# Activation transposes on TensorE in fp32, or by transposing DMAs of fp16 halves

## What is computed

```python
q = _layer_norm(query, ln1_g, ln1_b)
qh = (q @ wq + bq).reshape(Bq, Sq, H, hd)
kh = (context @ wk + bk).reshape(Bq, Sc, H, hd)
vh = (context @ wv + bv).reshape(Bq, Sc, H, hd)
scores = jnp.einsum('bqhd,bkhd->bhqk', qh, kh) / sqrt(hd)   # masked: key k only for query >= k
probs = jax.nn.softmax(scores, axis=-1)
o = jnp.einsum('bhqk,bkhd->bqhd', probs, vh).reshape(Bq, Sq, Dm)
x = query + o @ wo + bo
h = _layer_norm(x, ln2_g, ln2_b)
return x + jax.nn.gelu(h @ w1 + b1, approximate=False) @ w2 + b2
```

## Time and profile before

| | |
|---|---|
| median of three runs | 2116.74 us (2114.98 to 2117.86) |
| span of the profiled execution | 2112.4 us |
| median of the runs less that span | 4.3 us |
| TensorE busy | 1975.8 us (94% of the span) |
| VectorE busy | 1304.6 us (62%) |
| ScalarE busy | 589.0 us (28%) |
| GpSimd busy | 466.0 us (22%) |
| DMA moved | 51.30 MB, mean 24 GB/s |

### The profile page before, as it was taken

How to read it: one execution, slowest core, us unless ns; L and a number is a source line. 1 busy time by engine, 2 the same in 40 slices (tenths; PEclk the granted TensorE clock), 3 DMA queues, 4 the chain that set the end, 5 groups by cost and what they waited for, 6 DMA issues and landing times.

```text
span 2112.4 us, 26940 instructions
## 1 busy us (share of the span) xinstructions
PE 1975.8 (94%) x10454; PEld 1003.4 (47%) x10454; DVE 1304.6 (62%) x1972; ACT 589.0 (28%) x820; POOL 466.0 (22%) x380
## 2 busy tenths in 40 slices
PE   4769999999999999999999999999999999999999
PEld 2434445444454544545455444544444454454544
DVE  5876666655656675666666566666655667556642
ACT  3544323222232312223232222313223231222311
POOL 2530131311212141211412023131121214111110
PEclk9879999999999999999999999999999999999999
DMA  7210000101000010000101000010100001000000
GB/s 254 62 28 1 21 20 1 41 0 40 2 11 30 1 41 1 21 20 6 36 1 40 1 21 21 1 40 1 41 1 11 30 1 41 1 21 20 1 21 20
DMA packets 27647, 51.30 MB, mean 24 GB/s; under 512 B 2536, under 2 KB 4112, under 8 KB 27536
## 3 DMA queue, kind: packets, MB, share of 16 engines
q1 hardware_dynamic: 27536, 49.58, 7.1%
...
## 4 chain that ended last, share of the span: by engine, by line
PE 73%; DVE 16%; issue 5%; ACT 3%; DVEq 2%; DMA 0%; POOL 0%; SPq 0%; POOLq 0%; ACTq 0%
PE ff_ps L1190 25%; PE ff_ps L989 23%; PE at_ps L989 15%; PE at_ps L1109 4%; PE at_ps L1032 4%; DVE ssum L927 3%; DVE arena L962 3%; PE at_ps L1133 2%; DVE arena L711 2%; DVEq L688 2%; DVE xhat L707 2%; DVE act_T L711 1%; DVE arena L976 1%; ACT L590 1%; ACT arena L590 1%
## 5 line engine op out<-in xcount | busy, mean ns | idle before, releaser
L1190 PE MATMUL ff_ps<-w_all,arena 128*128 128x512 f16 x3072 | 707.4, 380 | 32.0 <-DVE arena L711 27.7
L989 PE MATMUL ff_ps<-arena,w_all 128*128 128x512 f16 x3072 | 708.5, 381 | 11.9 <-issue 10.3
L1190 PEld LDWEIGHTS ff_ps<-w_all,arena 128*128 128x128 f16 x3072 | 297.8, 98 | 374.2 <-DVE arena L711 30.3
L989 PEld LDWEIGHTS ff_ps<-arena,w_all 128*128 128x128 f16 x3072 | 299.9, 98 | 357.4 <-issue 26.7
L645 ACT ACTIVATE arena<-ff_ps,b1p,scales 128x512 f32<-128x512 f32 x256 | 199.1, 778 | 891.8 <-PE ff_ps L989 803.0
L711 DVE SCALAR_TENSOR_TENSOR arena<-arena,scales 128x512 f16<-128x512 f32 x256 | 285.2, 1114 | 9.1
L485 POOL TENSOR_TENSOR arena<-arena,rsum 128x1024 f32<-128x1024 f32 x64 | 122.7, 1948 | 723.3 <-DVE rsum L930 723.3
L421 POOL TENSOR_TENSOR rstd<-ve,minus_half 128x1 f32<-128x1 f32 x128 | 90.6, 708 | 709.7 <-DVE ve L692 701.4
L962 DVE TENSOR_SCALAR arena<-arena,scales 128x512 f16<-128x512 f32 x256 | 160.1, 625 | 69.3 <-ACT arena L645 69.3
L711 DVE SCALAR_TENSOR_TENSOR arena<-at_ps,arena 128x512 f16<-128x512 f32 x188 | 123.8, 686 | 110.8 <-ACT arena L596 58.5
L989 PE MATMUL at_ps<-wo_hi,act_T 128*128 128x512 f16 x512 | 162.3, 379 | 1.5 <-DVE act_T L711 1.5
...
## 6 DMA issues: line engine op xcount, KB each, us to landing
x_sb<-in_x SPq DMA_DIRECT2D x64, 256.0 KB, 2.6
out_x<-arena SPq DMA_DIRECT2D x64, 256.0 KB, 2.3
w_all<-in_L_xattn_w SPq DMA_DIRECT2D x6, 1024.0 KB, 14.8
arena<-in_L_xattn_w SPq DMA_DIRECT2D x2, 1024.0 KB, 15.0
v_sb<-v_sb SPq DMA_DIRECT2D x6, 192.0 KB, 3.0
arena<-in_ctx SPq DMA_DIRECT2D x1, 1024.0 KB, 5.5
arena<-in_L_xattn_wk SPq DMA_DIRECT2D x1, 1024.0 KB, 8.1
arena<-in_L_xattn_wv SPq DMA_DIRECT2D x1, 1024.0 KB, 8.0
```

The lines of the kernel that those rows point to most:

```text
L989: last = nc.tensor.matmul(out_ap, s, m, start=(i == 0), stop=(i == n - 1))
L1190: last = nc.tensor.matmul(ff2_ps[:, t, :], pair[:, s, rows], m[:, j], start=(j == 0 and i == 0), stop=(j == NJ - 1 and i == 2))
```

## The change

All 64 fp32 transposes of a slot (16 for T, 32 for Z, 16 for H) are taken off TensorE. T, Z and H now split the data where it lies, with tokens on the partitions, and a transposing DMA moves both halves at once:

- T and H: ScalarE copies `xhat` to the high half in `xhl[:, t, 0]`, VectorE subtracts it from `xhat` into `xhl[:, t, 1]`; then SP issues one `dma_start_transpose` of 128 tokens x 1024 fp16 columns (256 KB) into `act_T` or `hT`.
- Z: the same with `probs[t]`, 1024 columns to each half in `phl[:, t % 2]`, so one DMA of 128 tokens x 2048 fp16 columns (512 KB) a tile, written over `probs[t]` itself.
- `xhl` and `phl` share the memory of `qT`. `phl` has two buffers, so ScalarE's Z2 and Z3 wait for the moves of Z0 and Z1.
- SP waits for each low half, then issues the move; in program order stand four T moves, four Z moves, the x loads of tiles 0 to 2, the H move of tile 0, the x load of tile 3, the other H moves, and the output stores.
- TensorE waits for the moves: at Q0 for the four of T, at V0 and V2 for two of Z each, at FF1(0) of the next slot for the four of H.
- `xhat` is free again when VectorE has made its low half.
- The plan moves: T at 2, 3, 4, 5; Q from 7; S and E one later; Z at 20 to 23; V0 and V1 at 24, V2 and V3 at 26; O at 27 to 30; H at 30 to 33 as before but for H1 and H2, one later.

```diff
-    2: [("T", 0)], 4: [("T", 1)], 5: [("T", 2), ("T", 3)],
-    6: [("Q", 0)], 7: [("Q", 1)], 8: [("Q", 2)], 9: [("Q", 3)],
-    10: [("S", 0)], 12: [("S", 1)], 13: [("S", 2)], 15: [("S", 3)],
-    16: [("E", 0), ("E", 1), ("E", 2), ("E", 3)],
-    20: [("Z", 0)], 21: [("Z", 1)], 22: [("V", 0), ("V", 1)],
-    23: [("Z", 2)], 24: [("Z", 3)], 25: [("V", 2), ("V", 3)],
-    26: [("O", 0)], 27: [("O", 1)], 28: [("O", 2)], 29: [("O", 3), ("H", 0)],
-    30: [("H", 1)], 31: [("H", 2)], 33: [("H", 3)],
+    2: [("T", 0)], 3: [("T", 1)], 4: [("T", 2)], 5: [("T", 3)],
+    7: [("Q", 0)], 8: [("Q", 1)], 9: [("Q", 2)], 10: [("Q", 3)],
+    11: [("S", 0)], 13: [("S", 1)], 14: [("S", 2)], 16: [("S", 3)],
+    17: [("E", 0), ("E", 1), ("E", 2), ("E", 3)],
+    20: [("Z", 0)], 21: [("Z", 1)], 22: [("Z", 2)], 23: [("Z", 3)],
+    24: [("V", 0), ("V", 1)], 26: [("V", 2), ("V", 3)],
+    27: [("O", 0)], 28: [("O", 1)], 29: [("O", 2)], 30: [("O", 3), ("H", 0)],
+    31: [("H", 1)], 32: [("H", 2)], 33: [("H", 3)],
...
+            def move_normed(c, t):
...
+                sp.wait_ge(t_lo, 4 * c + t + 1)
+                sp.sem_inc(moves_begun, 1)
+                sp.dma_start_transpose(act_blocks[:, :, t * P:(t + 1) * P],
+                                       xhl[:, t].rearrange("p a n -> p (a n)")).then_inc(t_moved[t], 16)
+
+            def move_probs(c, t):
+
+                sp.wait_ge(z_lo, 4 * c + t + 1)
+                sp.sem_inc(moves_begun, 1)
+                sp.dma_start_transpose(pT_blocks[t],
+                                       phl[:, t % 2].rearrange("p a n -> p (a n)")).then_inc(z_moved[t], 16)
+
+            def move_hidden(c, par, t):
...
+                sp.wait_ge(h_lo, 4 * c + t + 1)
+                sp.sem_inc(moves_begun, 1)
+                sp.dma_start_transpose(hT_blocks[par][:, :, t * P:(t + 1) * P],
+                                       xhl[:, t].rearrange("p a n -> p (a n)")).then_inc(h_moved[t], 16)
...
+                if attn:
+                    if not first:
+                        for t in range(TT):
+                            move_normed(c, t)
+                    for t in range(TT):
+                        move_probs(c, t)
+                    for t in range(TT - 1):
+                        load_next(t)
+                    move_hidden(c, par, 0)
+                    load_next(TT - 1)
+                    for t in range(1, TT):
+                        move_hidden(c, par, t)
...
+                if kind == "T":
+                    act.wait_ge(ln_out, 8 * c + t + 1)
+                    wait(act, h_moved[t], 16 * c)
+                    nc.scalar.activation(xhl[:, t, 0], xhat[:, t % 2, :], ACT.Copy).then_inc(t_hi, 1)
...
+                    act.wait_ge(p_norm, 4 * c + t + 1)
+                    if t < 2:
+                        wait(act, z_moved[t + 2], 16 * c)
+                    else:
+                        act.wait_ge(z_moved[t - 2], 16 * c + 16)
+                    nc.scalar.activation(phl[:, t % 2, 0], probs[t], ACT.Copy, scale=PROB_SCALE).then_inc(z_hi, 1)
...
+                nc.vector.tensor_tensor(xhl[:, t, 1], xhat[:, t % 2, :], xhl[:, t, 0], ALU.subtract).then_inc(t_lo, 1)
...
-            def transposes(source, bank, done):
-                for k in range(KT):
-                    last = nc.tensor.transpose(bank[:, k * P:(k + 1) * P], source[:, k * P:(k + 1) * P],
-                                               ident[:, :])
-                last.then_inc(done, 1)
...
                         if t == 0:
-                            pe.wait_ge(t_lo, 4 * c + 4)
+                            for n in range(TT):
+                                pe.wait_ge(t_moved[n], 16 * c + 16)
...
+                        if t % 2 == 0:
+                            for n in range(2):
+                                pe.wait_ge(z_moved[t + n], 16 * c + 16)
...
                         if g == 0:
-                            pe.wait_ge(h_lo, 4 * c)
+                            for n in range(TT):
+                                pe.wait_ge(h_moved[n], 16 * c)
```

More of the change, by code:

```diff
@@ L381, in move_values @@
                     sp.dma_start(v_sb[SC:P, a, even, :], v_sb[0:SC, a, even, :]).then_inc(v_moved, 16)
+            def move_normed(c, t):
+                if t == 0:
+                    wait(sp, o_ps, 4 * c)
+                    sp.sem_inc(moves_begun, 1)
[9 more added lines that the diff above has]
+            def move_hidden(c, par, t):
+                if t == 0:
+                    wait(sp, ff1_done, NJ * c + (-NJ))
+                    sp.sem_inc(moves_begun, 1)
+                    if isinstance(c, int) and c == 1:
+                        sp.wait_ge(conv_lo, len(conversions))
+                sp.wait_ge(h_lo, 4 * c + t + 1)
+                sp.sem_inc(moves_begun, 1)
+                sp.dma_start_transpose(hT_blocks[par][:, :, t * P:(t + 1) * P],
+                                       xhl[:, t].rearrange("p a n -> p (a n)")).then_inc(h_moved[t], 16)
+            for t in range(2):
+                move_normed(0, t)
             move_values(0, slice(0, 2))
+            for t in range(2, TT):
+                move_normed(0, t)
             move_values(1, slice(2, BATCH))
@@ L388, in slot, with load_next @@
             def slot(c, par, attn, ff, batch):
-                if not isinstance(c, int) or c < NCHUNK - 1:
-                    for t in range(TT):
+                first = isinstance(c, int) and c == 0
+                loads = not isinstance(c, int) or c < NCHUNK - 1
+                def load_next(t):
+                    if loads:
                         sp.wait_ge(x1_set, 4 * c + t + 1)
                         sp.dma_start(x_sb[:, t], x_tiles[4 * c + (TT + t)]).then_inc(x_loaded[t], 16)
+                if attn:
[10 more added lines that the diff above has]
+                        move_hidden(c, par, t)
                 if ff:
@@ L907, in step @@
                         dve.wait_ge(h_hi, 4 * c + t + 1)
-                        rows = slice(t * P, (t + 1) * P)
-                        low(hT[par][:, 1, :, rows], tiles, 1.0, hT[par][:, 0, :, rows], h_lo)
+                        nc.vector.tensor_tensor(xhl[:, t, 1], xhat[:, t % 2, :], xhl[:, t, 0], ALU.subtract
+                                                ).then_inc(h_lo, 1)
                         if t < 2:
@@ L1052, in _ @@
                                              for k in range(KT)]).then_inc(kv_ps, 1)
-            for t in range(2):
-                T_step(0, t)
             pe.wait_ge(wv_out, KT)
```

113 lines of the change are left out of this document (40 added, 73 removed), and 4 rows, old and new, of the table PLAN_FIRST.

## The result

The kernel after takes 2150.3 us (median, 2144.4 to 2154.3) against 2117.3 us of before on the same chip: a ratio of 1.016, 95% interval 1.014 to 1.018. The forecast was slower by 5.7% (2238 us); it is slower by 1.6%. The sign came out and most of the mechanism, the size did not: of +121 us between the spans, +40 were there. The profiled span is 2152.6 us. Between the medians the difference is 33 us, less than the 40 between the spans, because the profiled execution of after is the slowest of its four (2154.3 us).

What follows compares the result with a forecast made beforehand. VectorE's chain and its handover at Q0 bound the kernel; odd slots 128.9 us (+5.6), even 136.0 (+8.9), seven pairs +101, slots 0 and 1 +13 and +8, last -1: +121, so 2238 us; own range 2170 to 2330, overall 2100 to 2430.

Steps and rivals of the forecast that it cites:

- X: Time of one T or H move with waits and wake-up: 4.6 us (2.85 to 8.5), of which 4.4 landing.
- Z: As a time, one move of the probabilities with waits and wake-up: 7.15 us (3.85 to 17), of which 6.9 landing.
- step 4: V0 and V2 wait for the Z moves through two buffers, together 7.5 us per slot.
- H3's move is hidden: Between O3 and Q0: VectorE's chain goes on under FF1(0)'s wait, so only T3's move delays Q0.
- What bounds the kernel: At the handover to Q0: TensorE is nearly full, but Q0 starts when VectorE's chain, ending with T3's low half, lets it.
- Removed work: On TensorE: 64 transposes, 7.0 us per slot, some 105 us in 15 slots; also FF2(8)'s wait of 1.93 us.
- rival A: Moves run as fast as HBM loads: 2093 us, or 2170 at an SBUF copy's pace; chance 0.20.
- its second price: Moves at an SBUF copy's pace, 3.75 us for T and H, 5.75 for the probabilities: 2170 us.
- The formula: Waits of V0 and V2 per slot: twice the probabilities' move time less 6.8 us, 7.5 us together.
- Clock: TensorE's idle stretches bring the lower clock level: 1.5 us per odd and 2.5 per even slot (bounds 0 and 5).
- The start and the end: Slot 0 +13 us (0 to 25), slot 1 +8 (0 to 12), last slot -1.
- rival B: Slow or queued moves on one queue, 7 us for T and H, 12 for the probabilities: 2451 us; chance 0.20.

Runs made afterwards that it cites:

- e4: after with matmuls whose result nobody reads ahead of FF1(0)'s wait (18) and Q0's (10): 2122.8 us, 1.004 of before.
- e6: after with Q, S and E one position later in the written order: 2194.9 us, 1.034 of before.
- e5: before with its transposes kept and only the written order of work changed to that of after: 2078.5 us, 0.982 of before.
- e1: after with T and H back on TensorE in fp32, only the probabilities (Z) moved by DMA: 2047.0 us, 0.968 of before.
- e12: after with every Z move issued twice in series: 2427.6 us, 1.147 of before.
- e8: after with H's last move (H3) issued twice in series: 2179.6 us, 1.030 of before.

## Why the prediction was right, and where it was wrong

The step that failed is the size of the moves, X and above all Z, and with it step 4, V's waits: 7.5 us per slot forecast, 1.2 and 2.1 measured. That alone is some 82 us in seven pairs of slots, and the forecast for the pairs was 82 us too high. A second step, "H3's move is hidden", failed as well; the shorter moves hid that in even slots.

**What bounds the kernel.** Right in even slots: VectorE's chain and the handover at Q0. T3's doubled move came out one to one at Q0 (3.2 us for 3.1), and Q0 stayed at 36.6 to 36.8 us when TensorE was filled (e4) or given more work ahead of it (e6). In odd slots TensorE counts as well: with the filler Q0 came 1.4 us earlier.

**Removed work.** Right: 3.5 of the 7.0 us of transposes per slot are seen from e5 to e1, with V's wait of 1 us against them, and the order gave 2.1 us where 1.98 were counted. The other 3.5 us, T's and H's, stood ahead of Q0, where after has TensorE wait.

**Moves.** The term that failed. X was taken as 4.4 us to land and Z as 6.9, a quarter above copies inside SBUF by a slope through 64 and 192 KB. Measured: T 3.1, H 3.2 (4.3 to 4.9 for the last two, which queue), Z 4.4. With the 0.25 us of waking that is X = 3.4 and Z = 4.65, between the point from which rival A decides (3.1 and 4.4, no change) and its second price at the pace of a copy inside SBUF (3.75 and 5.75, 2170 us), and the time, 2150, lies between theirs. The surcharge of a quarter for short pieces had no row behind it. The slope had two rows, but they are for 64 and 192 KB: from 256 to 512 KB the landing grew by 1.3 us, not by 2. The Trainium skill, "Advanced Engine Details and Errata", section "X-Bar Transpose (TRN2)", has transposing DMAs as fast as regular ones: by these rows nearly so, 3.1 us against 2.6 for 256 KB loaded from HBM. In the Trainium skill's "VectorE: DVE Perf Modes", "The three transpose paths" has 1309 ns for one 128x128 block; here eight blocks land in 3.1 us, 0.39 per block, the figure that it gives for TensorE. TensorE's own fp32 transposes took 0.11 us per block here (eight in 0.87).

**V's waits.** The other half of the same failure, and nearly the whole miss. From the end of one block of matmuls to the start of the next, V0 waits 0.9 us and V2 0.2 (odd) or 1.2 (even), so 1.2 and 2.1 per slot. The formula with the landing as measured, 2 x 4.65 - 6.8 = 2.5, comes near, and e12 shows that its shape is right. The text had said that it would be wrong if V waited less than 2 us; in odd slots it did.

**H and T.** FF1(0)'s wait was forecast at 5.3 us; it is 5.8 in even slots and 4.1 in odd ones. Q0 was forecast 36.65 us after O3 in even slots and came at 36.8; but this is luck, two errors that cancel, the move 1.2 us shorter and VectorE's chain 1.4 longer. In odd slots, 31.0 forecast, 32.7 measured, the chain is 2.9 longer. The step that failed here is "H3's move is hidden behind this chain": split 0 needs gelu 0, that needs FF1(0), and VectorE stands idle for it, 2.8 us in the even slot shown and 1.6 in the odd one. e8 shows it paid in full in odd slots and mostly given back in even ones. The low halves of T were to take over 1 us in even slots: in the slot shown only T0's did (1.64), the other three took 0.7.

**Clock.** Forecast 1.5 us per odd slot and 2.5 per even one. In odd slots Q0 to O3 is 89.7 us where the clock stays up and 90.5 in the mean, so 0.7 behind Q0, and by e4 1.4 before it. In even slots 89.3 + 2.1 = 91.4 would be without loss, and 93.3 were measured, so 1.9. The matmuls behind FF1(0) lose 2 us in even slots too, which cost nothing. The size was right, its place in odd slots was not: the sum below has 1.4 us of it under Q0.

**The start and the end.** Forecast +21 for the start, measured +16.8, of which the queue behind the 1 MB loads is some 4 that the forecast did not have. The last slot was forecast at -1 and came out at +4.0. The 4.3 us from span to median did not carry over: after's median is 2.3 us below its profiled span.

Sum: odd 128.9 + 1.7 (Q0 later) - 6.3 (V) - 0.8 (clock behind Q0) = 123.5, measured 123.1; even 136.0 + 0.2 - 5.4 - 0.6 = 130.2, measured 130.1. Seven pairs are then 78 us less than the forecast's +101, so +23, and +19.4 is what was measured. The forecast's own arithmetic has one slip, in rival B: its even slot adds up to 149.6 and not 149.9, which changes nothing here.
